# Attention stacks of a two-layer kernel: their transfers moved one slot later in the DMA queue's order of steps, projections one slot further ahead, six stack tiles for five, four node tiles for five

## What is computed

```python
x = x + attn(_layernorm(x), ...)                      # first layer: gated linear attention + MLP
nodes = {-1: _layernorm(x)}                           # second layer
for c in range(6):                                    # NUM_NOD
    nsrc = min(c + 1, 5); snode = c - nsrc            # MAX_PREV = 5
    in_q, in_k, in_v = (c - 1, snode, snode + nsrc // 2)
    q = ew[c, 0] * (nodes[in_q] @ We[eq] + be[eq])    # k and v alike, from in_k and in_v
    o = softmax((q @ Wq[c]) (k @ Wk[c]).T / 4) (v @ Wv[c]) @ Wo[c]      # 8 heads
    nodes[c] = act_w[c] * o + q
out = x + _layernorm(nodes[5]) * ln_g + ln_b
```

## Time and profile before

| | |
|---|---|
| median of three runs | 1064.5 us (1063.66 to 1065.46) |
| the profiled execution's own time | 1066.53 us |
| its span, first to last instruction | 1064.6 us, so 1.9 us lie around it |
| PE busy | 980.8 us, 92% of the span |
| DVE, ACT, POOL busy | 838.1, 723.3, 447.6 us |
| second layer, first to last slot start | 275.67 to 1045.24 us: 95 slots, 8.10 us each |

### The profile page before, as it was taken

How to read it: one execution, slowest core, us unless ns; L and a number is a source line. 1 busy time by engine, 2 the same in 40 slices (tenths; PEclk the granted TensorE clock), 3 DMA queues, 4 the chain that set the end, 5 groups by cost and what they waited for, 6 DMA issues and landing times.

```text
span 1064.6 us, 26783 instructions
## 1 busy us (share of the span) xinstructions
PE 980.8 (92%) x9705; PEld 699.2 (66%) x9705; DVE 838.1 (79%) x1805; ACT 723.3 (68%) x1601; POOL 447.6 (42%) x874
## 2 busy tenths in 40 slices
PE   8989999998799999999999999999999999999995
PEld 4765656555566766767666777667666676676763
DVE  5466777766689997878888899888788888888896
ACT  3345666665577777777677778877777777777775
POOL 3522222233343344335444448843443344443365
PEclk9889999999899999999999999999999999999998
DMA  9100000006466666666676676576566666657641
GB/s 234 27 1 1 1 0 0 0 2 87 64 108 99 99 92 105 97 104 96 102 107 92 102 105 113 109 117 102 94 107 98 101 97 104 104 93 106 103 74 35
DMA packets 72407, 87.33 MB, mean 82 GB/s; under 512 B 11642, under 2 KB 45950, under 8 KB 72286
## 3 DMA queue, kind: packets, MB, share of 16 engines
q1 hardware_dynamic: 70686, 83.69, 48.8%
q0 software_dynamic: 800, 1.98, 0.8%
q10 hardware_dynamic: 800, 0.05, 0.0%
HBM read 6.90 MB, written 2.10 MB: 8 GB/s over the span
## 4 chain that ended last, share of the span: by engine, by line
PE 38%; DMA 20%; DVE 11%; ACT 9%; SPq 8%; POOL 6%; issue 6%; DVEq 0%; POOLq 0%; ACTq 0%
PE bank L1288 37%; DMA mst<-mrows 19%; SPq L503 8%; ACT region L816 4%; POOL hl L591 3%; POOL hl L588 3%; DVE region L1154 2%; DVE region L1086 1%; ACT qk L781 1%; ACT qk L780 1%; DVE region L970 1%; DVE region L1081 1%; ACT region L792 1%; PE bank L1624 1%; DVE region L1074 1%
## 5 line engine op out<-in xcount | busy, mean ns | idle before, releaser
L1154 DVE TENSOR_REDUCE region<-bank 128x2 f32<-128x512 f32 x768 | 489.3, 680 | 120.2 <-PE bank L1288 119.7
L816 ACT ACTIVATE region<-bank 128x512 f32<-128x512 f32 x768 | 406.5, 599 | 68.0 <-PE bank L1288 65.2
L1288 PE MATMUL bank<-st 48*128 48x256 f32 x3072 | 309.6, 326 | 5.3 <-DVE region L1154 4.5
L588 POOL TENSOR_TENSOR hl<-qk,one_col 128x512 fp32r<-128x512 f32 x96 | 100.1, 1043 | 395.0 <-ACT qk L781 395.0
L1288 PEld LDWEIGHTS bank<-st 48*128 48x128 f32 x3072 | 243.1, 189 | 19.7 <-DVE region L1154 5.3
L1288 PE MATMUL bank<-region 128*32 128x256 f32 (+3 forms) x3554 | 250.0, 377 | 2.7 <-DVE region L1181 1.0
L1288 PEld LDWEIGHTS bank<-region 128*32 128x32 f32 (+2 forms) x3554 | 130.7, 117 | 86.1 <-issue 17.0
L1288 PE MATMUL bank<-mst,ones 64*128 64x512 bf16 x768 | 150.1, 387 | 37.2 <-DMA mst<-mrows 34.3
L591 POOL TENSOR_TENSOR hl<-qk,hl 128x512 fp32r<-128x512 f32 x96 | 122.9, 1280 | 7.5
L838 ACT ACTIVATE mrows<-bank 24x256 bf16<-24x256 bf16 x96 | 35.8, 373 | 128.6 <-PE bank L1624 128.6
L1288 PEld LDWEIGHTS bank<-mst,ones 64*128 64x128 bf16 x768 | 37.0, 92 | 97.8 <-DMA mst<-mrows 51.9
(11 more groups left out here) (193 smaller groups left out, 1269.6 us busy)
## 6 DMA issues: line engine op xcount, KB each, us to landing
st<-hl SPq DMA_DIRECT2D x576, 128.0 KB, 4.3
out<-xall POOLq DMA_DIRECT2D x14, 128.0 KB, 3.7
mst<-mrows SPq DMA_DIRECT2D x96, 12.0 KB
xall<-in_L_attn_hidden_states SPq DMA_DIRECT2D x1, 768.0 KB, 7.0
cst<-in_constants SPq DMA_DIRECT2D x1, 514.5 KB, 3.9
xT<-in_L_ffn_Wq SPq DMA_DIRECT2D x1, 384.0 KB
xT<-in_L_ffn_Wk SPq DMA_DIRECT2D x1, 384.0 KB
xT<-in_L_ffn_Wv SPq DMA_DIRECT2D x1, 384.0 KB
```

The source lines that it names most:

```text
L588: pool.tensor_tensor(to[:, K_HI::Q_HI - K_HI, :], qk[a.n % 2], one_col[:, :].unsqueeze(2).to_broadcast([P, 2, T]), ALU.mult)\
L816: act.activation(to, x_bank(x, k, e)[:, :].rearrange("p (j q) -> p j q", j=2), ACT.Exp).then_inc(B["exp_ok"], 1)
L1154: dve.tensor_reduce(mx[s.n % 2][:, to:to + 2], s_bank(s, k, e)[:, :].rearrange("p (j k) -> p j k", j=2), AX_X, ALU.max, negate=True).then_ ...
L1288: return pe.matmul(o, w, x, start=start, stop=stop, skip_group_check=skip)
```

## The change

The constants that place the stages shift by one: scores are read three slots behind the projection instead of two, and every later stage moves with them. SP's `phase` issues, behind the maxima of slot t, the stacks of step t-1 instead of t. One more slot (`EARLY` 4) is woven into the end of the first layer. A step's stack now lives one slot longer, so there are six stack tiles; to make room, the first five nodes of a sequence share four tiles (node 4 takes the place of node 1, whose last reader comes before it). The table `RING`, which gives PSUM banks to scores and weights, is rotated so that each slot meets the same banks as before.

```diff
-S_AT, M_AT, X_AT, D_AT, Z_AT, W_AT, V_AT = 2, 3, 4, 5, 6, 7, 8
+S_AT, M_AT, X_AT, D_AT, Z_AT, W_AT, V_AT = 3, 4, 5, 6, 7, 8, 9
-STACKS = 5
+STACKS = 6
-RING = ((4, 5), (0, 1), (2, 6))
+RING = ((0, 1), (2, 6), (4, 5))
-EARLY = 3
+EARLY = 4
+NODE_AT = (0, 1, 2, 3, 1)
-        UW = 22760
+        UW = 20128
-        node = carve(LIVE, NODES - 1, T)
+        node = carve(LIVE, NODES - 2, T)
...
             def phase(t, a, s, m, x, d, z, w, v):
                 if m is not None:
                     maxima_rows(m)
-                if a is not None:
-                    stack(a)
+                if at_slot(t, 1) is not None:
+                    stack(at_slot(t, 1))
...
                 if f is None and i is None:
+                    phase(*stages(3))
                     return
...
                     if last:
-                        scores(stages(2)[2], 2)
+                        scores(stages(3)[2], 2)
+                        project_qk(stages(3)[1])
                     mlp_out(j)
                     if last:
-                        scores(stages(2)[2], 3)
+                        scores(stages(3)[2], 3)
...
-                if old is None and t == EARLY:
+                if old is None and place(t, kind, k) % len(RING) < 2:
                     pe.wait_ge(B["max_ok"], UNITS)
```

More of the change, by code:

```diff
@@ L820, in copy_node @@
                 act.wait_ge(B["node_ps"].sem, B["node_ps"].at(z.n))
-                act.activation(node[:, z.lb, z.c, :], bank[OUT][:, T:2 * T], ACT.Identity, bias=bcol[:, z.c, 2:3])\
+                act.activation(node[:, z.lb, NODE_AT[z.c], :], bank[OUT][:, T:2 * T], ACT.Identity, bias=bcol[:, z.c, 2:3])\
                     .then_inc(B["node_ok"], 1)
@@ L944, in first @@
                     if k is None:
-                        maxes(stages(2)[2], 0)
+                        maxes(stages(3)[2], 0)
                     times_up(j, 0)
@@ L948, in first @@
                     if k is None:
-                        maxes(stages(2)[2], 1)
+                        maxes(stages(3)[2], 1)
                 if k is not None:
@@ L995, in first @@
                     if f is None and i is None and k is None:
-                        maxes(stages(2)[2], 2)
-                        maxes(stages(2)[2], 3)
+                        maxes(stages(3)[2], 2)
+                        maxes(stages(3)[2], 3)
                 if i is not None:
@@ L1367, in first @@
                     if last:
-                        scores(stages(2)[2], 0)
+                        scores(stages(3)[2], 0)
                         project_qk(stages(2)[1])
@@ L1373, in first @@
                     if last:
-                        scores(stages(2)[2], 1)
+                        scores(stages(3)[2], 1)
                     pe.wait_ge(A["hid_ok"], j * MT + 1)
@@ L1478, in source @@
             def source(s, n):
-                return xT[:, s.f * T:s.f * T + T] if n < 0 else node[:, s.lb, n, :]
+                return xT[:, s.f * T:s.f * T + T] if n < 0 else node[:, s.lb, NODE_AT[n], :]
             def project_qk(a):
```

## The result

The changed kernel takes 1026.45 us (median of 4 runs, 1024.41 to 1026.53) against 1064.08 us before (4 runs, 1063.26 to 1065.46): a ratio of 0.964, 95% interval 0.9624 to 0.9657. The profiled execution took 1026.44 us, 40.1 less than the one before; executions differ by some microseconds in the first layer, by when the granted clock rises (over the first 100 us its mean was 0.88 in the one before, 0.90 in this one and 0.93 in that of experiment 9, whose second layer also began 4 us sooner), while kernels whose second layer should be equal agree in its length within 0.5 us (730.2, 730.4 and 730.2 us, and 726.3 twice, in the table of experiments).

A forecast was written before the change was run, and what follows sets the result against it. PE was taken to bound the second layer, losing 34.3 us waiting for the maxima's DMA. 34.3 - 1.0 - 1.6 - 2.1 - 0.6 = 29.0 us gain, so 1064.5 - 29.0 = 1035.5 us; range 1028 to 1048.

The forecast's parts named there:

- The mechanism: Second layer: the maxima travel behind the stacks, in issue and in flight; with stacks moved, all 34.3 us of waits go.
- the signs named in advance: SP waits for ACT's `mrows` in nearly every slot, plain slots take 7.7 us, last-node slots 8.1, ACT's `qk` releases POOL's split.
- The arithmetic of the flight: Maxima issued at 612.95 land at 614.8 if alone; PE wants them at 617.15: 2.3 us slack, 1.9 in shorter slots.
- term (a): PE's work per slot swells without pauses, 7.60 to 7.72 us; 0.1 us for some ten slots, 1.0 us lost.
- Theory P: Expectation of the runs with two and three stacks ahead: a pause costs 0.07 us more than its idle row.
- rival Q: PE in the same runs: slots begun without a pause work 7.7 us, after a long one 7.6; no chance given.
- (b): Slots with first-layer statistics: DVE becomes the bound, about five slots by about 0.3 us, 1.6 us lost.
- (c): Last-node slots: a loop through POOL's norm and store keeps its 8.13 us period, so 2.1 us of waits stay.
- The row of 34.3 us: Table of waits: PE's waits for the DMA of the maxima, 58 of them, all counted as gain.
- Term (d): The layer's ends: an added 1.03 us projection at the start, 0.4 counted back at the far end; 0.6 us lost.
- Rival 2: More is won: (a) to (d) cost nothing and PE holds 7.60 instead of 7.68 us in 80 slots; 1024 us, 5%.
- The third rival: A DMA of `mrows` takes some 4.1 us whatever lies ahead, so almost no gain: 1064 us, 4%.

The follow-up runs named there:

- experiment 9: Changed kernel with the fourteen stores of finished sequences issued by SP behind the slot's stacks instead of by POOL, and five stack tiles instead of six: 1022.79 us.
- experiment 1: Changed kernel, but SP again issues the stacks of slot t's own step behind its maxima; scores stay three slots behind the projection: 1063.28 us.
- experiment 6: Changed kernel, but SP issues two of the six stack DMAs before the maxima and the rest behind them: 1086.77 us.
- experiment 7: Changed kernel, but SP issues three of the six stack DMAs before the maxima and the rest behind them: 1223.02 us.
- experiment 4: Changed kernel with the fourteen stores of finished sequences issued by SP behind the slot's stacks instead of by POOL: 1023.43 us.
- experiment 8: Kernel before the change, but ACT issues the DMA of the maxima behind its own copy and SP issues only stacks: 1093.95 us.
- experiment 2: Kernel before the change, but SP issues the stacks of step t-1 behind slot t's maxima; scores stay two slots behind the projection: 1658.80 us.
- experiment 5: Changed kernel, but SP issues one of the six stack DMAs before the maxima and the rest behind them: 1025.21 us.

## Why the prediction came out too high

**The mechanism was right.** The maxima were late by SP's issue and by the stacks ahead of them, all the waits for them went, and the signs named in advance are there: SP waits for ACT in 96 steps, last-node slots stay at 8.1 us, `hl` does not bind. The arithmetic of the flight holds as well: landing expected at 614.8 in the old time frame, with 1.9 us of slack in shorter slots; measured 2.2.

**The step that failed is term (a)**, "PE's own work swells a little without pauses", 1.0 us lost. It has the wrong sign: for the same 8171 matmuls, PE's drawn busy time is 3.4 us shorter without the pauses (726.6 us in experiment 1, 723.2 after), an error of 4.4 us. I compared 7.72 and 7.60 us of the earlier trace rows as if both were work; but the longer one is the slot that *ends* in a pause (its window also reaches 0.03 us into the next slot). No matmul takes longer there: one of the last group takes 274 ns in the mean, before, after and in experiment 6. But the modelled end of the last one is covered by its successor when there is one, and counts in full when PE pauses. Take the piece before the slot's end in the two timelines: in the changed kernel the last four matmuls begin at 590.66 and the next slot at 591.20, 0.54 us later. With the pause of experiment 6, of which the last line here is a whole slot,

```profile
586.93 0.61 PE L1300 MATMUL bank<-w_fold,region 128*128 128x128 f32 x4
588.22 0.39 PE L1300 MATMUL bank<-mst,ones 64*128 64x512 bf16 x2 [0.69 <-DMA mst<-mrows]
...
588.22:596.47 8.25, 7.68 (x87) 5.62 (x88) 6.60 (x12) 5.94 (x13) 3.01 (x7) 1.00 0.55 97
```

1.29 us lie between them, of which the trace calls 0.69 idle: 1.29 - 0.54 = 0.75 is what the pause costs, 0.06 more than its row. Theory P of experiments 6 and 7 holds, and rival Q, the prediction's own reading, is refuted: at full clock a plain slot with a pause is busy 7.68 us whether the pause is 0.6 us or 1.6, and 7.61 without one. So a removed pause gives back its idle time and some 0.07 us. Over the layer this adds up: outside the slots of (b) and (c), 59 slots of experiment 1 end in a pause and are 3.8 us busier together than in the changed kernel; in those of (b) and (c), PE's drawn busy time is 0.4 us longer in the changed kernel.

**Waits that my row did not hold.** The row of 34.3 us was not all of the late maxima. At the slots' starts PE was idle for 37.2 us before, and for nothing after. In eight of these starts, 2.35 us together, the table names DVE, in this row:

```profile
PE bank L1288 <- DVE region L1154: 6.9, 12, 1.9
```

(its other four waits are not at a slot's start). The trace settles whose pauses they were: by the semaphore events PE starts 0.05 us after the maxima have landed in all 76 starts with a pause, these eight included. So 2.9 us more were to be won.

**Terms (b) and (c), other engines.** The eight slots with statistics took 66.6 us before (324.15 to 390.78) and 65.2 after (320.49 to 385.64): 1.5 us won where the pauses that ended them summed to 2.3, so 0.8 did not come back, where (b) had 1.6. The eight last-node slots took 64.7 us before (642.02 to 706.72) and 65.1 after (621.78 to 686.85), although their pauses of 2.2 us went: 2.6 for (c), where the prediction had 2.1. So (b) was too large, and (c) right in mechanism and slightly small; experiment 4 shows the store to be the cause. Outside the slots' starts PE's idle time in the layer grew by 2.3 us, from 4.7 to 7.0, where (b) and (c) had 3.7.

**Term (d), the ends, 0.6.** From the projection of the earlier trace rows to the first slot's start it was 25.28 us before (250.39 to 275.67) and 25.75 after:

```profile
249.27 1.03 PE L1292 MATMUL bank<-xT,w_fold 128*128 128x256 f32 x4
```

0.5 us longer, where the projection's 1.03 were charged; in return the layer's busy time is some 1.0 us shorter, where 0.4 were counted back. What lies outside the layer is 295.0 us of the span before and 294.4 after; the difference of the whole first layer is of the size by which its executions vary (the layer began between 270.7 and 277.0 us in the runs of this study).

**The sum.** In the layer, 30.0 us were forecast (29.0, and the 1.0 of the projection that is charged outside it), and 39.4 found. Of the 9.4 between them, 4.4 are (a), 2.9 the pauses that another row held, 1.4 the idle time that (b) and (c) were charged too much, and 0.6 the projection in (d). By medians the whole kernel gained 37.6 instead of 40.0 of the two spans, since the profiled execution before was 2.4 us above its median. **Rival 2** ("more is won", 1024) was the nearest. Its price of a plain slot, 7.60 us instead of 7.68, is what was measured, while (b) and (c) did cost something. I gave it 5% because I had read term (a) the wrong way round.

**The rule weighed.** The third rival, that the maxima's flight is their own, is refuted: 1.87 us with no stack issued shortly before them, 2.9 to 4.4 with some. The fit in the Trainium skill, page "DMA: Bandwidth & Descriptors", section "Anatomy of one DMA — SWDGE (gpsimd) path", gives 2.0 us for 12 KB, close to the 1.87 us here, although it is stated for the other path. It is no guide to a DMA behind others. On experiment 8 the Trainium skill, same page, section "Issuing engines are not separate DMA queues", says that DMAs of all issuers run on the same 16 DMA engines and interleave; the trace agrees in so far as ACT's own queue did not shield the maxima (4.39 us). The Trainium skill, same page, section "Queues, rings and completion order", says more: an engine takes turns between queues packet by packet, by which alone one would expect the maxima to overtake most of the stacks; and a semaphore's increment lands only after the engine's earlier writes, across queues, by which they would land about when the stacks do. The landings, half of them within 0.14 us of the last stack's on either side, fit the second better, but no run separates the two.

## What to carry to other kernels

A small transfer that is on the critical path should find no large one issued shortly ahead of it; giving it a queue of its own did not help here, issuing the large ones behind it did, if what reads them can wait a slot longer. Test the lead and the order separately, since here each without the other was worth nothing or less. When you count the pauses that one late event causes, look at every start that it can delay, not only at the row that names it. And when you price pauses from a trace, add up the period between two starts of the same instruction, with and without a pause, instead of idle rows and busy times: the drawn end of the last instruction hides a part of each pause.

## What the runs showed of the hardware

- A DMA of 12 KB took 1.87 us (median) from issue to landing with no stack of 128 KB under way (experiment 2), and the same when two or three of the slot before were still under way that landed, as a rule, before it (the changed kernel). It took 2.9, 3.5 and 3.8 us behind one, two and three DMAs of 128 KB just issued (experiments 5 to 7), and 4.4 us from another engine's queue, mostly with four to six under way (experiment 8).
- The price of recurring pauses depends on their length. With 0.7 us a slot PE's granted clock stayed at 1.00 (experiment 6). With 1.6 us it fell in 30 of 95 slots, to a mean of 0.84 in the one shown (experiment 7). With 4 to 5 us it was 0.80 over the layer, and PE's busy time rose from 727.6 to 952.2 us (experiment 2).
- Issuing a DMA cost the issuer's queue, but for a few, 0.74 to 0.82 us on ACT and POOL. Where that queue sets the length of a slot, each such slot pays for it (8.17 us against 7.68 with the store moved off POOL, experiment 4); with 96 issues on ACT the kernel was 30 us slower (experiment 8).
